# An LSTM step's first half packed into 128 columns of PSUM, and the second half's o + 1 moved to GpSimd

## Chip, core and metric

One core of one Trainium2 chip. The metric is device time in microseconds of the whole kernel: 1992.09 us, the median of three runs (1990.87 to 1992.61).

## What is computed

Input x is 8 sequences of 512 steps and 512 features. An LSTM runs over them and is added to x; a small state space model (a conditioned convolution over the eight last steps, a gated scan with 64 states, a projection back) runs over the result and is added again.

```python
def step(carry, xw_t):                    # 512 times, H = 512, batch 8
    prev_h, prev_c = carry
    a = xw_t + prev_h @ Wh                # Wh: 512 x 2048
    i = sigmoid(a[:, :H]); f = sigmoid(a[:, H:2*H]); o = sigmoid(a[:, 2*H:3*H])
    g = tanh(a[:, 3*H:])
    next_c = f * prev_c + i * g
    next_h = o * tanh(next_c)
x = x + lstm(x, h0=cond[:, :512], Wx, Wh, b)
proj = (conv_b + causal_conv(x, taps=cond)) @ Wp + bp
state_t = decay * state + dt * softplus(proj[..., :64]) * (x @ Ws + bs)
x = x + (tanh(proj[..., 64:]) * state_t) @ Wo + bo
```

## The kernel before

The 512 steps of the LSTM are a chain: each needs the h of the one before. Everything else (the projection of x by Wx, the convolution, the scan, the output) is cut into small jobs that are written into the steps, beside the chain. Plain Python lists fix ahead of time which job stands in which step (`project_at`, `conv_when`, `post_at`, `out_when`); every engine then executes its own instructions strictly in the order written, and semaphores join them.

One step splits the 512 hidden units into four chunks of 128 and these into two halves: half 0 (called A, bank recA, chunks 0 and 1) and half 1 (B, recB, chunks 2 and 3). Each half goes through the same stages:

- ScalarE (`seeds`, L626) writes the projected x of the step into the PSUM bank, scaled by a mask that keeps the rows of this step and sets the others to zero. Two steps lie in one row of `seed`.
- TensorE (`recur`, L465) adds h @ Wh. h is the stationary operand, 16 columns: 8 sequences times a high and a low f16 part (they fill 16 rows). Wh moves, also split into a high and a low part (`whi`, `wlo`), 256 columns at a time (two chunks of 128). The 128 rows of the bank are four quadrants of 32, one for each j; in each quadrant 16 rows are used and 16 are empty. For each chunk k of the previous h there are 2 x 4 = 8 matmuls per half, so 32 in a half and 64 in a step. The order of the step is A k=0, A k=1, B k=0, A k=2, A k=3, B k=1, 2, 3. Chunks 0 and 1 wait for the previous step's h of half A (`s_h[0]`), chunks 2 and 3 for that of half B (`s_h[1]`); the first also waits for the seed.
- VectorE transposes blocks of 32 x 32 (`open_`, L812: 128 x 256), adds the rows of the high and low part of h (`add`, L818), and later forms i * g and f * c (`product`, L823) and c (`cell`, L828).
- ScalarE makes tanh of all gates (`gates`, L699; the sigmoid is taken from tanh) and tanh of c (`tanh_c`, L709).
- o + 1 times a constant: for half A on GpSimd (L400), for half B on ScalarE (`opened`, L705).
- GpSimd multiplies it by tanh of c, h in f32 (L406). VectorE makes the high f16 part of h (`high`, L834) and, from GpSimd's h, the low part (`low`, L840), which releases the next step's matmuls.

The orders within a step, which the engines keep:

```python
# VectorE (then beside(t))
open_(t, 0); add(t, 0); open_(t, 1); product(t, 0); add(t, 1); cell(t, 0)
product(t, 1); high(t, 0); cell(t, 1); low(t, 0); high(t, 1); low(t, 1)
# ScalarE (then beside(t))
gates(t, 0); seeds(t + 1, 0); gates(t, 1); tanh_c(t, 0); opened(t); seeds(t + 1, 1); tanh_c(t, 1)
```

TensorE runs its beside(t) after all 64 matmuls of the step: L435 and L432 (projection), L510 (convolution), L483, L523, L530 (output). The DMA queue of SyncE brings the projected rows back from a scratch in HBM (`rows_back`, L336), four transfers for each tile and half.

The functions in full:

Of the kernel before, what the change touches and what calls it, by code (L numbers as in the profile page):

```python
# [5 lines left out]
def lstm_ssm_kernel(nc: bass.Bass, x, cond, Wx, Wh, b, conv_b, Wp, bp, Ws, bs, A_log, dt_log, Wo, bo, out):  # L6
    f32 = mybir.dt.float32
    f32r = mybir.dt.float32r
    f16 = mybir.dt.float16
    bf16 = mybir.dt.bfloat16  # L10
    i32 = mybir.dt.int32
    ALU = mybir.AluOpType
# [19 lines left out]
    with ctx:  # L32
# [18 lines left out]
        mask = sb("mask", [128, 2])  # L51
        yt = sb("yt", [128, XR, KC, ROW])
        h32 = sb("h32", [128, KC, HS, NB])
        hb = [sb(f"hb{i}", [128, KC, 2 * NB], f16) for i in range(2)]
        h0b = [sb(f"h0b{i}", [128, KC, 2 * NB], bf16) for i in range(2)]
# [18 lines left out]
        tr = [sb(f"tr{h}", [128, 2, G, 4, NB]) for h in range(2)]  # L74
# [82 lines left out]
        brow = [xs[z:z + 1, :, :].rearrange("p c n -> p (c n)") for z in (0, 32)]  # L157

# [151 lines left out]
        def _(sync):  # L310
# [14 lines left out]
            def rows_back(g, c, z):  # L325
# [8 lines left out]
                back = scratch[g % 2, c, :, :].rearrange("(t q) (j f) -> j q t f", q=2 * NB, j=4)  # L334
                for j in range(4):
                    sync.dma_start(seed[32 * j:32 * j + 2 * NB, z, :, c // 2, 128 * (c % 2):128 * (c % 2) + 128],  # L336
                                   back[j, :, TS // 2 * z:TS // 2 * z + TS // 2, :]).then_inc(s_seedin[z], 16)
# [43 lines left out]
        def _(pool):  # L381
# [16 lines left out]
            for t in range(T):  # L398
                pool.wait_ge(s_tg[0], t + 1)
                pool.tensor_scalar(osc[0][:, :], act[0][:, 2, :], 1.0, SC, ALU.add, ALU.mult).then_inc(s_os[0], 1)  # L400
                for q in range(2):
                    pool.wait_ge(s_tc[q], t + 1)
# [8 lines left out]
        def _(pe):  # L411
# [43 lines left out]
            def recur(t, half, k):  # L455
# [6 lines left out]
                for h in (h0b if t == 0 else [hb[(t - 1) % 2]]):  # L462
                    for w in (whi, wlo):
                        for j in range(4):
                            ins = pe.matmul(rec[half][32 * j:32 * j + 2 * NB, 0:256].rearrange("p (c f) -> p c f", c=2),  # L465
                                            h[:, k, :],
                                            w[:, k, :, :].rearrange("p (c j) f -> p c j f", j=4)[:, 2 * half:2 * half + 2, j, :],
                                            start=False, stop=(k == KC - 1), skip_group_check=True)
# [123 lines left out]
        def _(act_eng):  # L592
# [29 lines left out]
            def seeds(t, q):  # L622

                if t % TS == 0 and q == 0:
                    act_eng.wait_ge(s_seedin[t // TS % 2], 256 * (t // TT + 1))
                act_eng.activation(rec[q][:, 0:256], seed[:, t // TS % 2, t % TS // 2, q, :],  # L626
                                   ACT.Copy, scale=mask[:, t % 2:t % 2 + 1]).then_inc(s_seed[q], 1)
# [74 lines left out]
            def opened(t):  # L702

# [380 lines left out]
```

## Time and profile before

| what | value |
|---|---|
| median of three runs | 1992.09 us |
| the profiled execution's own time | 1992.87 us |
| its span | 1991.0 us |
| mean granted TensorE clock | 0.987 of 2.4 GHz |
| PE busy | 1791.8 us, 90%, 36290 matmuls |
| VectorE busy | 1430.1 us, 72%, 6913 instructions |
| ScalarE busy | 1043.9 us, 52%, 4056 instructions |
| GpSimd busy | 349.4 us, 18%, 1546 instructions |

The busy times are of one execution. Matmuls are pipelined, the time of one reaches from its start to its last result, and those of neighbours overlap, so 90% isn't a full engine. Four matmuls that go to the four quadrants start almost at once and stand in the timeline as one row, "x4". PE, PEld, DVE, ACT and POOL are matmuls, weight loads, VectorE, ScalarE and GpSimd. An idle time in brackets at the end of a row names what ended it.

### The profile page before, as it was taken

What the parts mean: (1) busy time and instruction counts of PE and PEld (TensorE: products, weight loads), DVE (VectorE), ACT (ScalarE), POOL (GpSimd) and SP (SyncE); (2) the same over time, 40 slices, a digit from 0 to 9 for tenths busy, and PEclk for the clock granted to TensorE, in tenths of its full rate; (3) what the DMA queues carried; (4) which work ended last, traced back from release to release, by engine and by line L of the source; (5) the groups of instructions that cost most, each with busy time, mean ns of one, the idle gap of its engine ahead of it and who ended that gap; (6) DMA issues with size and microseconds to landing.
All of it is one profiled execution on the core that took longest, in us unless ns stands there. A gap on an engine that the chain in (4) does not pass through costs nothing.

```text
span 1991.0 us, 90455 instructions
## 1 busy us (share of the span) xinstructions
PE 1791.8 (90%) x36290; PEld 1282.6 (64%) x36290; DVE 1430.1 (72%) x6913; ACT 1043.9 (52%) x4056; POOL 349.4 (18%) x1546
## 2 busy tenths in 40 slices
PE   2688899999999999999999999999999999999976
PEld 1455666666666666666666666766666677666755
DVE  4577666777777777777767777777777777767775
ACT  3355555555555555555555555555555555555452
POOL 3011111111111111111111111111111111111110
PEclk8799999999999999999999999999999999999998
DMA  5111111111121111111111111111111111211100
GB/s 201 49 47 44 39 50 36 40 55 48 37 61 49 42 45 51 49 41 58 46 48 46 44 46 51 53 49 49 46 39 51 50 52 34 66 45 40 47 17 23
DMA packets 112284, 98.71 MB, mean 50 GB/s; under 512 B 20097, under 2 KB 86197, under 8 KB 110838
## 3 DMA queue, kind: packets, MB, share of 16 engines
q1 hardware_dynamic: 111490, 92.35, 15.3%
q8 instruction: 286, 4.69, 1.0%
q14 instruction: 134, 1.10, 0.2%
q10 hardware_dynamic: 374, 0.57, 0.1%
HBM read 50.90 MB, written 41.94 MB: 47 GB/s over the span
## 4 chain that ended last, share of the span: by engine, by line
PE 45%; DVE 33%; ACT 11%; issue 5%; POOL 4%; DMA 1%; SPq 0%; ACTq 0%; POOLq 0%; DVEq 0%
PE recA L465 25%; DVE tr L812 16%; PE recB L465 9%; DVE pre L818 7%; ACT act L699 5%; PE pw L435 5%; PE pbc L510 5%; POOL h L406 4%; DVE hb L840 3%; ACT tc L709 3%; DVE prod L823 2%; DMA xs<-in_L_cond_b_dram 1%; ACT recB L626 1%; DVE acc L893 1%; DVE st L914 0%
## 5 line engine op out<-in xcount | busy, mean ns | idle before, releaser
L699 ACT ACTIVATE act<-pre 128x64 f32<-128x64 f32 x1024 | 262.8, 257 | 874.0 <-DVE pre L818 857.6
L465 PE MATMUL recA<-whi,hb 128*16 128x256 f16 x8176 | 514.6, 274 | 137.8 <-DVE hb L840 131.3
L465 PE MATMUL recB<-wlo,hb 128*16 128x256 f16 x8176 | 513.2, 273 | 0.0
L465 PE MATMUL recB<-whi,hb 128*16 128x256 f16 x8176 | 513.2, 273 | 0.0
L465 PE MATMUL recA<-wlo,hb 128*16 128x256 f16 x8176 | 512.9, 273 | 0.0
L465 PEld LDWEIGHTS recA<-whi,hb 128*16 128x16 f16 x8176 | 200.0, 88 | 402.8 <-DVE hb L840 347.1
L812 DVE STREAM_TRANSPOSE tr<-recA 128x256 f32<-128x256 f32 x512 | 229.9, 449 | 215.5 <-PE recA L465 214.3
L510 PE MATMUL pbc<-yt,wpk 128*128 128x256 f32 (+5 forms) x1120 | 333.7, 402 | 0.0
L406 POOL TENSOR_TENSOR h<-osc,tc 128x16 f32<-128x16 f32 x1024 | 227.8, 222 | 500.8 <-ACT tc L709 500.8
L400 POOL TENSOR_SCALAR osc<-act 128x16 f32<-128x16 f32 x512 | 105.0, 205 | 1088.3 <-ACT act L699 1088.3
L823 DVE SCALAR_TENSOR_TENSOR prod<-act 128x32 f32<-128x32 f32 x1024 | 196.7, 192 | 126.4 <-ACT act L699 126.4
L818 DVE TENSOR_TENSOR pre<-tr 128x64 f32<-128x64 f32 x1024 | 229.3, 224 | 17.6
L626 ACT ACTIVATE recA<-seed,mask 128x256 f32<-128x256 f32 x512 | 236.1, 461 | 9.2 <-DMA seed<-xw_rows 9.2
L834 DVE TENSOR_TENSOR hb<-osc,tc 128x16 f16<-128x16 f32 x1024 | 178.1, 174 | 85.2 <-ACT tc L709 83.7
L626 ACT ACTIVATE recB<-seed,mask 128x256 f32<-128x256 f32 x512 | 236.1, 461 | 0.0
L435 PE MATMUL pw<-wxh,xh 128*128 128x512 f32 x504 | 228.0, 452 | 6.6 <-DVE wxl L785 5.8
L812 DVE STREAM_TRANSPOSE tr<-recB 128x256 f32<-128x256 f32 x512 | 230.0, 449 | 1.8 <-PE recB L465 1.8
L840 DVE TENSOR_TENSOR hb<-h,hb 128x16 f16<-128x16 f32 x1024 | 179.5, 175 | 70.8 <-POOL h L406 3.7
L510 PEld LDWEIGHTS pbc<-yt,wpk 128*128 128x128 f32 x1120 | 169.9, 190 | 90.6 <-issue 85.8
L435 PE MATMUL pw<-wxh,xl 128*128 128x512 f32 x504 | 219.6, 436 | 0.0
L465 PEld LDWEIGHTS recB<-wlo,hb 128*16 128x16 f16 x8176 | 204.7, 90 | 19.2
L465 PEld LDWEIGHTS recB<-whi,hb 128*16 128x16 f16 x8176 | 204.7, 90 | 19.1
(150 smaller groups left out, 2051.7 us busy)
## 6 DMA issues: line engine op xcount, KB each, us to landing
xw_rows<-xs SPq DMA_DIRECT2D x128, 256.0 KB, 2.1
seed<-xw_rows SPq DMA_DIRECT2D x1024, 32.0 KB, 1.9
out_dram<-ot SPq DMA_DIRECT2D x32, 256.0 KB, 3.0
xn<-in_x_dram SPq DMA_DIRECT2D x30, 256.0 KB
seed<-in_L_cond_Wh_dram SPq DMA_DIRECT2D x2, 1024.0 KB, 7.3
wpk<-in_L_cond_Wh_dram SPq DMA_DIRECT2D x2, 1024.0 KB, 14.7
wlo<-in_L_cond_Wx_dram SPq DMA_DIRECT2D x2, 1024.0 KB, 20.2
xs<-in_L_cond_Wx_dram SPq DMA_DIRECT2D x1, 1024.0 KB, 4.9
```

The lines of the kernel that those rows point to most:

```text
L400: pool.tensor_scalar(osc[0][:, :], act[0][:, 2, :], 1.0, SC, ALU.add, ALU.mult).then_inc(s_os[0], 1)
L406: pool.tensor_tensor(h32[:, 2 * q:2 * q + 2, t % HS, :], osc[q][:, :].rearrange("p (c b) -> p c b", c=2), tc[q][:, :].rearrange("p (c b) - ...
L435: pe.matmul(out, xx[:, g % 2, k, :], wxm[w][:, k, c, :, :, :], start=(first and part == 0), stop=False)
L465: ins = pe.matmul(rec[half][32 * j:32 * j + 2 * NB, 0:256].rearrange("p (c f) -> p c f", c=2), h[:, k, :], w[:, k, :, :].rearrange("p (c j ...
L510: ins = pe.matmul(pbc[:, NB * (lo - a):NB * (hi - a)], wpk[:, k, c, :], yt[:, n % XR, c, NB * (lo + k):NB * (hi + k)], start=(j == 0), sto ...
L626: act_eng.activation(rec[q][:, 0:256], seed[:, t // TS % 2, t % TS // 2, q, :], ACT.Copy, scale=mask[:, t % 2:t % 2 + 1]).then_inc(s_seed[ ...
L699: act_eng.activation(act[q][:, 0:G, :].rearrange("p g n -> p (g n)"), pre[q][:, :, :, :].rearrange("p g c b -> p (g c b)"), ACT.Tanh, scal ...
L812: dve.transpose(tr[q][:, :, :, :, :].rearrange("p c g z b -> p (c g z b)"), rec[q][:, 0:256]).then_inc(s_tr[q], 1)
L818: dve.tensor_tensor(pre[q][:, :, :, :].rearrange("p g c b -> p c g b"), tr[q][:, :, :, 0, :], tr[q][:, :, :, 1, :], ALU.add).then_inc(s_ad ...
L823: dve.scalar_tensor_tensor(prod[q][:, :, :], act[q][:, 0:2, :], 1.0, act[q][:, 3:5, :], ALU.add, ALU.mult).then_inc(s_prod[q], 1)
L834: dve.tensor_tensor(hb[t % 2][:, 2 * q:2 * q + 2, 0:NB], osc[q][:, :].rearrange("p (c b) -> p c b", c=2), tc[q][:, :].rearrange("p (c b) - ...
L840: dve.tensor_tensor(hb[t % 2][:, 2 * q:2 * q + 2, NB:2 * NB], h32[:, 2 * q:2 * q + 2, t % HS, :], hb[t % 2][:, 2 * q:2 * q + 2, 0:NB], ALU ...
```

## The change

Half A's two chunks now share a quadrant: chunk c = 0 takes rows 0 to 15 and c = 1 rows 16 to 31, in the same 128 columns. To write one chunk and add nothing to the other's rows, the stationary operand becomes 32 columns wide: h with 16 columns of zeros behind it (c = 0) or ahead of it (c = 1). `hz` and `h0z` hold 16 zero columns on both sides of h for that, and `hb`, `h0b` are now views of their middle. Half A then takes 4 x 2 x 2 x 4 = 64 matmuls of 128 columns (before 32 of 256); half B keeps its 32 of 256. That makes 96 in a step.

With it half A's seed and transpose are 128 columns wide (`WIDTH`), its mask keeps other rows, the transfers that bring the seed back place chunk 1 in rows 16 to 31, and the add reads another order. The o + 1 of half B moves from ScalarE (`opened`, which is gone) to GpSimd, between h of A and h of B. Lines without a change are cut from the diff.

```diff
@@ -48,11 +48,12 @@
         seed = sb("seed", [128, 2, TS // 2, 2, 256])
-        mask = sb("mask", [128, 2])
+        mask = sb("mask", [128, 2, 2])
         yt = sb("yt", [128, XR, KC, ROW])
         h32 = sb("h32", [128, KC, HS, NB])
-        hb = [sb(f"hb{i}", [128, KC, 2 * NB], f16) for i in range(2)]
-        h0b = [sb(f"h0b{i}", [128, KC, 2 * NB], bf16) for i in range(2)]
+        hz = [sb(f"hz{i}", [128, KC, 6 * NB], f16) for i in range(2)]
+        h0z = [sb(f"h0z{i}", [128, KC, 6 * NB], bf16) for i in range(2)]
         h0f = sb("h0f", [128, 2, KC, NB])
@@ -71,7 +72,7 @@
         scale = sb("scale", [128, 4])
-        tr = [sb(f"tr{h}", [128, 2, G, 4, NB]) for h in range(2)]
+        tr = [sb("tr0", [128, G, 2, 2, NB]), sb("tr1", [128, 2, G, 4, NB])]
         pre = [sb(f"pre{h}", [128, G, 2, NB]) for h in range(2)]
@@ -155,6 +156,10 @@
+        hb, h0b = ([h[:, :, 2 * NB:4 * NB] for h in hs] for hs in (hz, h0z))
+        WIDTH = (128, 256)
@@ -332,8 +337,9 @@
                 back = scratch[g % 2, c, :, :].rearrange("(t q) (j f) -> j q t f", q=2 * NB, j=4)
+                row, col = ((2 * NB * c, 0), (0, 128 * (c % 2)))[c // 2]
                 for j in range(4):
-                    sync.dma_start(seed[32 * j:32 * j + 2 * NB, z, :, c // 2, 128 * (c % 2):128 * (c % 2) + 128],
+                    sync.dma_start(seed[32 * j + row:32 * j + row + 2 * NB, z, :, c // 2, col:col + 128],
                                    back[j, :, TS // 2 * z:TS // 2 * z + TS // 2, :]).then_inc(s_seedin[z], 16)
@@ -396,9 +402,10 @@
             for t in range(T):
-                pool.wait_ge(s_tg[0], t + 1)
-                pool.tensor_scalar(osc[0][:, :], act[0][:, 2, :], 1.0, SC, ALU.add, ALU.mult).then_inc(s_os[0], 1)
                 for q in range(2):
+                    pool.wait_ge(s_tg[q], t + 1)
+                    pool.tensor_scalar(osc[q][:, :], act[q][:, 2, :], 1.0, SC, ALU.add, ALU.mult).then_inc(s_os[q], 1)
                     pool.wait_ge(s_tc[q], t + 1)
@@ -459,13 +466,22 @@
-                for h in (h0b if t == 0 else [hb[(t - 1) % 2]]):
-                    for w in (whi, wlo):
-                        for j in range(4):
-                            ins = pe.matmul(rec[half][32 * j:32 * j + 2 * NB, 0:256].rearrange("p (c f) -> p c f", c=2),
-                                            h[:, k, :],
-                                            w[:, k, :, :].rearrange("p (c j) f -> p c j f", j=4)[:, 2 * half:2 * half + 2, j, :],
-                                            start=False, stop=(k == KC - 1), skip_group_check=True)
+                for h in (h0z if t == 0 else [hz[(t - 1) % 2]]):
+                    if half:
+                        for w in (whi, wlo):
+                            for j in range(4):
+                                ins = pe.matmul(rec[1][32 * j:32 * j + 2 * NB, 0:256].rearrange("p (c f) -> p c f", c=2),
+                                                h[:, k, 2 * NB:4 * NB],
+                                                w[:, k, :, :].rearrange("p (c j) f -> p c j f", j=4)[:, 2:4, j, :],
+                                                start=False, stop=(k == KC - 1), skip_group_check=True)
+                    else:
+                        for c in range(2):
+                            for w in (whi, wlo):
+                                for j in range(4):
+                                    ins = pe.matmul(rec[0][32 * j:32 * j + 32, 0:128],
+                                                    h[:, k, 2 * NB * (1 - c):2 * NB * (1 - c) + 32], w[:, k, 4 * c + j, :],
+                                                    start=False, stop=(k == KC - 1), skip_group_check=True)
                 if k == KC - 1:
@@ -623,8 +639,8 @@
                     act_eng.wait_ge(s_seedin[t // TS % 2], 256 * (t // TT + 1))
-                act_eng.activation(rec[q][:, 0:256], seed[:, t // TS % 2, t % TS // 2, q, :],
-                                   ACT.Copy, scale=mask[:, t % 2:t % 2 + 1]).then_inc(s_seed[q], 1)
+                act_eng.activation(rec[q][:, 0:WIDTH[q]], seed[:, t // TS % 2, t % TS // 2, q, 0:WIDTH[q]],
+                                   ACT.Copy, scale=mask[:, q, t % 2:t % 2 + 1]).then_inc(s_seed[q], 1)
@@ -699,11 +715,6 @@
-            def opened(t):
-                act_eng.wait_ge(s_tg[1], t + 1)
-                act_eng.activation(osc[1][:, :], act[1][:, 2, :], ACT.Copy, bias=SC, scale=SC).then_inc(s_os[1], 1)
@@ -748,7 +759,7 @@
             act_eng.wait_ge(s_bits, 2)
-            act_eng.wait_ge(s_mask, 5)
+            act_eng.wait_ge(s_mask, 7)
             for q in range(2):
@@ -758,7 +769,6 @@
                     tanh_c(t, 0)
-                    opened(t)
                     if t + 1 < T:
@@ -809,14 +819,18 @@
                 dve.wait_ge(s_rec[q], t + 1)
-                dve.transpose(tr[q][:, :, :, :, :].rearrange("p c g z b -> p (c g z b)"),
-                              rec[q][:, 0:256]).then_inc(s_tr[q], 1)
+                order = ("p g c z b -> p (g c z b)", "p c g z b -> p (c g z b)")[q]
+                dve.transpose(tr[q][:, :, :, :, :].rearrange(order), rec[q][:, 0:WIDTH[q]]).then_inc(s_tr[q], 1)
                 dve.wait_ge(s_tr[q], t + 1)
-                dve.tensor_tensor(pre[q][:, :, :, :].rearrange("p g c b -> p c g b"), tr[q][:, :, :, 0, :],
-                                  tr[q][:, :, :, 1, :], ALU.add).then_inc(s_add[q], 1)
+                if q:
+                    dve.tensor_tensor(pre[1][:, :, :, :].rearrange("p g c b -> p c g b"), tr[1][:, :, :, 0, :],
+                                      tr[1][:, :, :, 1, :], ALU.add).then_inc(s_add[1], 1)
+                else:
+                    dve.tensor_tensor(pre[0][:, :, :, :], tr[0][:, :, :, 0, :],
+                                      tr[0][:, :, :, 1, :], ALU.add).then_inc(s_add[0], 1)
@@ -966,8 +980,8 @@
                 dve.memset(act[q][:, 4, :], 0.0).then_inc(s_c[q], 1)
-                dve.memset(hb[q][:, :, :], 0.0)
-                dve.memset(h0b[q][:, :, :], 0.0).then_inc(s_hz, 1)
+                dve.memset(hz[q][:, :, :], 0.0)
+                dve.memset(h0z[q][:, :, :], 0.0).then_inc(s_hz, 1)
             dve.memset(ones[:, :].bitcast(f32), 1.0).then_inc(s_hz, 1)
@@ -975,7 +989,9 @@
             for z in range(2):
-                dve.tensor_reduce(mask[:, z:z + 1], diag[:, z:16:4], mybir.AxisListType.X, ALU.max).then_inc(s_mask, 1)
+                for q in range(2):
+                    dve.tensor_reduce(mask[:, q, z:z + 1], diag[:, z:16:2 + 2 * q], mybir.AxisListType.X,
+                                      ALU.max).then_inc(s_mask, 1)
@@ -1009,7 +1025,7 @@
             dve.wait_ge(s_max, KC + 1)
-            dve.wait_ge(s_mask, 3)
+            dve.wait_ge(s_mask, 5)
             dve.tensor_scalar(diag[:, :], ident[:, :], top[:, 4:5], None, ALU.mult).then_inc(s_max, 1)
@@ -1030,8 +1046,8 @@
             dve.wait_ge(s_scale, 1)
-            for z in range(2):
-                dve.tensor_scalar(mask[:, z:z + 1], mask[:, z:z + 1], scale[:, 2:3], None, ALU.mult).then_inc(s_mask, 1)
+            for q in range(2):
+                dve.tensor_scalar(mask[:, q, :], mask[:, q, :], scale[:, 2:3], None, ALU.mult).then_inc(s_mask, 1)
             wh_high(2)
```

## Rows read from the trace of the kernel before

**Rows 1.** The page: chain by line, then two groups (busy us, mean ns of one).

```profile
PE recA L465 25%; DVE tr L812 16%; PE recB L465 9%; DVE pre L818 7%; ACT act L699 5%; PE pw L435 5%; PE pbc L510 5%; POOL h L406 4%; DVE hb L840 3%; ACT tc L709 3%; DVE prod L823 2%; DMA xs<-in_L_cond_b_dram 1%; ACT recB L626 1%; DVE acc L893 1%; DVE st L914 0%
...
L465 PEld LDWEIGHTS recA<-whi,hb 128*16 128x16 f16 x8176 | 200.0, 88 | 402.8 <-DVE hb L840 347.1
...
L400 POOL TENSOR_SCALAR osc<-act 128x16 f32<-128x16 f32 x512 | 105.0, 205 | 1088.3 <-ACT act L699 1088.3
```

**Rows 2.** Chain in order of time, one step (start us, us, what).

```profile
1011.24 0.46 DVE tr L812
...
1011.95 0.40 DVE tr L812
```

**Rows 3.** Timeline of that step, PE (start us, us, engine, line, operation).

```profile
1009.92 0.29 PE L465 MATMUL recA<-whi,hb 128*16 128x256 f16 x4
...
1010.47 0.28 PE L465 MATMUL recB<-wlo,hb 128*16 128x256 f16 x4
1010.56 0.10 PEld L465 LDWEIGHTS recA<-whi,hb 128*16 128x16 f16 x4
1010.58 0.28 PE L465 MATMUL recA<-whi,hb 128*16 128x256 f16 x4
...
1010.91 0.28 PE L465 MATMUL recA<-wlo,hb 128*16 128x256 f16 x4
...
1011.56 0.28 PE L465 MATMUL recB<-wlo,hb 128*16 128x256 f16 x4
```

**Rows 4.** Same timeline, the other engines, to the next step's weights.

```profile
1011.24 0.45 DVE L812 STREAM_TRANSPOSE tr<-recA 128x256 f32<-128x256 f32 x1 [0.73 <-PE recA L465]
...
1011.73 0.22 DVE L818 TENSOR_TENSOR pre<-tr 128x64 f32<-128x64 f32 x1
...
1011.90 0.45 DVE L812 STREAM_TRANSPOSE tr<-recB 128x256 f32<-128x256 f32 x1
...
1012.15 0.46 ACT L626 ACTIVATE recA<-seed,mask 128x256 f32<-128x256 f32 x1
...
1012.38 0.22 DVE L818 TENSOR_TENSOR pre<-tr 128x64 f32<-128x64 f32 x1
1012.53 0.17 DVE L828 SCALAR_TENSOR_TENSOR act<-prod 128x16 f32<-128x16 f32 x1
...
1012.64 0.26 ACT L699 ACTIVATE act<-pre 128x64 f32<-128x64 f32 x1
...
1012.80 0.20 ACT L709 ACTIVATE tc<-act 128x16 f32<-128x16 f32 x1
1012.93 0.22 ACT L705 ACTIVATE osc<-act 128x16 f32<-128x16 f32 x1
...
1013.05 0.46 ACT L626 ACTIVATE recB<-seed,mask 128x256 f32<-128x256 f32 x1
1013.08 0.22 POOL L406 TENSOR_TENSOR h<-osc,tc 128x16 f32<-128x16 f32 x1 [0.55 <-ACT tc L709]
...
1013.34 0.18 DVE L840 TENSOR_TENSOR hb<-h,hb 128x16 f16<-128x16 f32 x1
1013.45 0.20 ACT L709 ACTIVATE tc<-act 128x16 f32<-128x16 f32 x1
1013.57 0.10 PEld L465 LDWEIGHTS recA<-whi,hb 128*16 128x16 f16 x4 [0.63 <-DVE hb L840]
```

**Rows 5.** Timeline where step 0 begins, PE.

```profile
72.91 0.13 PEld L465 LDWEIGHTS recA<-whi,h0b 128*16 128x16 bf16 x4 [10.90 <-issue]
72.94 0.39 PE L465 MATMUL recA<-whi,h0b 128*16 128x256 f16 x4 [10.49 <-ACT recA L626]
```

**Rows 6.** Timeline of the last stage, PE.

```profile
1972.62 0.69 PE L483 MATMUL pu<-yt,ws 128*64 128x64 f32 x16 [0.83 <-DVE yt L849]
1973.23 4.08 PE L510 MATMUL pbc<-yt,wpk 128*128 128x8 f32 x32
```

**Rows 7.** Waits of the whole run (us in total, times, longest us).

```profile
DVE tr L812 <- PE recA L465: 214.3, 453, 13.1
```

## The prediction

> **What bounds the kernel now.** I read the page's chain first, then the same chain in order of time, then the timeline of one plain step, and last the groups by form. The page gives the recurrence's matmuls into recA 25% of the chain, the transpose of L812 16%, recB 9% [rows 1]. In order of time one step reads: recA's matmuls, transpose A, add A, transpose B [rows 2]. Taken at its word, transpose A (0.46 us a step) sits on the path, and the change halves it. Whether it does sit there is the main question of this case.
>
> The timeline answers it. Call the first matmul of a step 0; it is 1009.92, and the next step's weight load is at 1013.57, so a step lasts 3.65 us. PE works in groups of four matmuls (j = 0 to 3) that start together, one group each 0.109 us: from 1010.58 to 1011.56 are nine intervals, 0.98 us [rows 3]. The order is A (chunks 0, 1), B (0), A (2, 3), B (1 to 3). The last A group starts at 1010.91 and runs 0.28, to 1011.19; transpose A starts at 1011.24, 0.05 later. The last B group starts at 1011.56, ends at 1011.84, and transpose B starts at 1011.90, 0.06 later [rows 3, 4]. Both transposes lag the end of their own matmuls by the same hand-over. Transpose B starts before add A has ended (1011.73 + 0.22 = 1011.95), 0.17 after add A started; VectorE can do that in 0.15 (add B 1012.38, cell A 1012.53) [rows 4]. So transpose B waits for PE, and the path of a step is: all sixteen groups (1.64 to the start of the last one, 0.28 for it), hand-over 0.06, transpose B 0.45, add B, gates B, tanh of c A (behind gates B on ScalarE; cell A, 1012.53 + 0.17 = 1012.70, was ready 0.10 before it), h of A on GpSimd, low part of A, next step's weights: 1011.90, 1012.38, 1012.64, 1012.80, 1013.08, 1013.34, 1013.57 [rows 4]. Transpose A and add A lie beside the B matmuls with about 0.02 us to spare (0.17 against 0.15). The chain view names them because they come just before transpose B on the same engine.
>
> **The change part by part.**
>
> *PE, first half.* Before: 8 groups of 256 columns, 8 x 0.109 = 0.872 us. After: 16 groups of 128 columns. The group of 256 columns takes 256 / 2.4 GHz = 0.107 us at the upper of TensorE's two clocks, and the rows show 0.109, so 0.0023 us come with each group. With 128 columns that is 0.0533 + 0.0023 = 0.0556 us, an estimate, and 16 of them are 0.890: 0.018 us longer in each step. The columns streamed are the same, the group's fixed part is paid twice. Bounds for the group, which the trace doesn't show for four tiles of 128 columns: below, 0.0533 (no fixed part, 0.019 us a step less than now); above, 0.109 as now (each matmul keeps its slot whatever its width, 0.872 us a step more). Which is nearer? The four matmuls of a group start within 0.01 us of each other and the four weight loads together take 0.10 us where one takes 0.09 [rows 1, 3], so tiles don't queue behind each other. The sixteen 64-column matmuls of L483, in pairs of two tiles, took 0.69 us with the last one's 0.23 in it: 0.46 us / 7 = 0.066 us a pair [rows 6]. So a group of well under 0.109 exists, and I take 0.0556.
>
> *Weight loads of 32 columns instead of 16.* 32 loads of 128-column weights with 8-column matmuls (where nothing but the weight can bind) took 4.08 us, 0.127 us each or about 0.032 us per 32 columns [rows 6]; a load starts while the group before streams. 0.032 is under 0.0556, so it is hidden, if the four tiles load side by side, as above. Only the first group of a step, which finds an idle array, shows it: 0 to 0.032, I take 0.007. Cost at nothing otherwise; if the four loads were serial the group would be 4 x 0.032 = 0.128, worse than the upper bound.
>
> *PE's queue.* 192 instead of 128 instructions (weights and matmuls) for a step's recurrence. The sequencer is free to run ahead from the seed of A on (that is the wait ahead of the first weights): seed A 1012.15 + 0.46 = 1012.61, the next weights 1013.57, 0.96 us ahead [rows 4]; after the change the seed ends about 0.2 earlier. In step 0, where the seed comes last, eight instructions start within 0.04 us of the first weight load [rows 5], 0.005 us each. Needed are eight per 0.0556, 0.007 each. I take no cost; the other end is the second rival.
>
> *VectorE.* Transpose A falls from 128x256 to 128x128. It took 0.45; the add with 64 columns takes 0.22 [rows 4], so 192 columns make 0.23 and 128 make 0.15, and about 0.30 is left. It lay beside the B matmuls, so this brings nothing in a plain step: next late is transpose B, which PE holds. In 512 - 453 = 59 steps VectorE came late to transpose A [rows 7]; there the shorter one gives back up to 0.15 each, 8.9 us at most, and since most of these are late by less or are late elsewhere too, I take 3 us. Add A has the same 64 results, only another order of reading: 0.22 as before.
>
> *ScalarE.* The seed of A falls by some 0.1 us, and the Copy that makes o + 1 of B (0.22, 1012.93) goes. Neither is on the path: A's tanh of c comes ahead of both the Copy and seed B. What moves is B's tanh: seed B starts 0.12 earlier (it followed the Copy at 1013.05), and then c of B is what is late. That makes B's h up to 0.1 us earlier; but PE takes chunks 2 and 3 at 1010.58, exactly one group interval (0.11) after the group at 1010.47 [rows 3], so B's h wasn't waited for. Gain 0. Bounds: 0 to -0.02, since it was just in time.
>
> *GpSimd.* It now makes o + 1 of B after h of A: h A ends 1013.08 + 0.22 = 1013.30, the new one (0.205 as its twin for A [rows 1]) then ends at about 1013.55. B's tanh, then 0.12 earlier than 1013.45, ends near 1013.55 as well. Behind the new wait on GpSimd stands h of B, and its low part and recA's chunks 2 and 3 wait for that. If o + 1 came 0.1 later than I have it, the high part would be where it is now. Cost 0, other end 0.05.
>
> *The rest.* DMAs keep their number and size. Masks, memsets (192 instead of 64 columns) and waits ahead of step 0 lie beside loads of Wx. 0, at most 1 us.
>
> **Sum**, against the profiled run's own 1992.87 us (span 1991.0): 512 x (0.018 + 0.007) = +12.8, late steps -3, in all +10, 2003. The median of the runs shown is 0.8 lower, so 2002 us.
>
> **A rule of the skill against this change.** The rows show four matmuls starting within 0.01 us [rows 3], and 0.109 / 4 = 0.027 us on average. The Trainium skill, TensorE: Matmul & The Clock Gate, "Wait — 56ns, not 53.3ns?", says that starts of consecutive matmuls are never less than about 25 ns apart however narrow they are. By that rule a group of four would take 0.100 us, an estimate from that page, and the change would cost 16 x 0.100 - 0.872 = 0.73 us a step, some 370 us. This case's starts inside a group contradict it as a spacing, but its average would just fit, so it stays as the third rival. The same page's "Part 3: Packing small matmuls" has tiles starting about 4 ns apart, and there the rows agree.
>
> **The rivals.**
> 1. *VectorE's order was the bound.* Then transpose A was on the path, as [rows 2] reads, and 0.15 x 512 = 77 us go: 1915. Against it: transpose B's 0.06 behind recB's end, and 0.17 where 0.15 does. It decides only if transpose B could start before PE is done, which it can't. Milder: the fixed part of a group vanishes at 128 columns and the late steps give all: 512 x -0.019 - 5 = -15 us, 1977.
> 2. *PE's sequencer can't feed the packed half.* If an instruction costs 0.0125 us (a little under the 0.109 / 8 = 0.0136 at which it is consumed now) and the queue holds what A's chunks 0 and 1 need, the 80 instructions from B's chunk 0 to A's last leave from about 0.22 us on, when the first have ended: 0.22 + 80 x 0.0125 = 1.22, needed at 1.06. That is 0.16 us a step, 82 us: 2074. Against it: the burst of [rows 5]. It decides from 0.0105 us an instruction.
> 3. *Each matmul keeps its slot.* Group 0.109: 0.872 us x 512 = 446 us, 2438. For it: nowhere in the trace are matmuls denser than 0.027 each on average. Against it: 64-column pairs, and the starts within a group.
> 4. *Nothing to be measured* (within 0.2%, 4 us, about what a measurement of this kernel can tell): the group at 0.054 to 0.055 or late steps giving more.
>
> **How the numbers follow.** Forecast (slower by 4 to 45 us) 0.52; rival 4 0.14; rival 1 in both forms 0.16; rival 2 and anything like it 0.12; rival 3 0.06. Faster 0.16, same 0.14, slower 0.52 + 0.12 + 0.06 = 0.70. The range reaches from the mild form of rival 1 to rival 2, 1978 to 2076, and leaves out the strong form of rival 1 and rival 3, with 0.09 and 0.06, and something of the edges. The forecast's own range is 1996 to 2037: its upper end is a group of 0.058 with 0.03 for the first one's weights.
>
> **What would show it right or wrong.** A's groups 0.055 to 0.056 apart; the last B group starting 1.66 to 1.67 after the step's first; transpose B still 0.05 to 0.06 behind recB's end, transpose A at about 0.30 with VectorE idle behind add A; a plain step of 3.67 to 3.68; h A, low A and the next weights at the same distances as in [rows 4]. Wrong would be: A's groups at 0.1 (rival 3), gaps in the second half of recA (rival 2), transpose B starting earlier than now counted from the step's first matmul (rival 1), or GpSimd's new o + 1 ending what h B waits for.

## The result, and the profile after

The changed kernel takes 2007.1 us, median of 4 runs (2006.48 to 2008.14); the kernel before takes 1991.48 us, median of 4 (1989.47 to 1992.61; the three runs shown and one more beside the changed kernel). The ratio is 1.0076, interval 1.0064 to 1.0089: slower, by 15 us. The forecast was 2002.0, slower, and the range of 1978 to 2076 holds the time.

The profiled execution after took 2008.14 us with a span of 2006.3, against 1992.87 and 1991.0 before: 15.3 us more. A plain step, as the median distance between the first matmuls of two steps, is 3.676 us, where it was 3.650. The last 511 steps make 0.026 x 511 = 13.3 of the 15.3.

The page after, its chain and three groups of it:

```profile
PE recA L482 26%; PE recB L474 22%; DVE tr L823 8%; PE pw L442 5%; PE pbc L526 5%; ACT act L715 5%; POOL h L413 4%; DVE pre L829 4%; DVE hz L854 3%; ACT tc L720 2%; DVE prod L837 2%; DMA xs<-in_L_cond_b_dram 1%; PE po L546 0%; PE po L539 0%; DVE acc L907 0%
...
L482 PE MATMUL recA<-whi,hz 128*32 128x128 f16 x16352 | 582.4, 220 | 137.8 <-DVE hz L854 131.3
L482 PEld LDWEIGHTS recA<-whi,hz 128*32 128x32 f16 x16352 | 404.3, 96 | 396.2 <-DVE hz L854 351.1
...
L408 POOL TENSOR_SCALAR osc<-act 128x16 f32<-128x16 f32 x1024 | 207.8, 203 | 1071.6 <-ACT act L715 1028.5
```

The chain names recB with 22% and the transposes with 8%, where it was 9% and 16% [rows 1]. That looks like work which moved from VectorE to TensorE. It isn't: experiment 3, below, shows the same exchange with no change in time. GpSimd's o + 1 now stands with 1024 instructions instead of 512.

The timeline of a plain step after, all engines, to the second half's high part in the next step:

```profile
1009.37 0.10 PEld L482 LDWEIGHTS recA<-whi,hz 128*32 128x32 f16 x4 [1.50 <-DVE hz L854]
1009.38 0.24 PE L482 MATMUL recA<-whi,hz 128*32 128x128 f16 x4 [1.09 <-DVE hz L854]
...
1009.44 0.23 PE L482 MATMUL recA<-wlo,hz 128*32 128x128 f16 x4
...
1009.50 0.23 PE L482 MATMUL recA<-whi,hz 128*32 128x128 f16 x4
...
1009.83 0.28 PE L474 MATMUL recB<-whi,hz 128*16 128x256 f16 x4
...
1010.05 0.23 PE L482 MATMUL recA<-whi,hz 128*32 128x128 f16 x4
...
1010.44 0.23 PE L482 MATMUL recA<-wlo,hz 128*32 128x128 f16 x4
...
1010.72 0.32 DVE L823 STREAM_TRANSPOSE tr<-recA 128x128 f32<-128x128 f32 x1 [0.35 <-PE recA L482]
...
1011.04 0.28 PE L474 MATMUL recB<-wlo,hz 128*16 128x256 f16 x4
1011.07 0.22 DVE L832 TENSOR_TENSOR pre<-tr 128x64 f32<-128x64 f32 x1
...
1011.38 0.45 DVE L823 STREAM_TRANSPOSE tr<-recB 128x256 f32<-128x256 f32 x1
1011.49 0.36 ACT L642 ACTIVATE recA<-seed,mask 128x128 f32<-128x128 f32 x1
...
1011.86 0.23 DVE L829 TENSOR_TENSOR pre<-tr 128x64 f32<-128x64 f32 x1
...
1012.12 0.26 ACT L715 ACTIVATE act<-pre 128x64 f32<-128x64 f32 x1 [0.27 <-DVE pre L829]
...
1012.28 0.20 ACT L720 ACTIVATE tc<-act 128x16 f32<-128x16 f32 x1
...
1012.57 0.22 POOL L413 TENSOR_TENSOR h<-osc,tc 128x16 f32<-128x16 f32 x1 [0.69 <-ACT tc L720]
...
1012.82 0.18 DVE L854 TENSOR_TENSOR hz<-h,hz 128x16 f16<-128x16 f32 x1
1012.85 0.22 ACT L720 ACTIVATE tc<-act 128x16 f32<-128x16 f32 x1
1012.87 0.20 POOL L408 TENSOR_SCALAR osc<-act 128x16 f32<-128x16 f32 x1
1013.05 0.10 PEld L482 LDWEIGHTS recA<-whi,hz 128*32 128x32 f16 x4 [0.37 <-DVE hz L854]
...
1013.18 0.18 DVE L848 TENSOR_TENSOR hz<-osc,tc 128x16 f16<-128x16 f32 x1 [0.18 <-POOL osc L408]
```

Read it against [rows 3, 4]. A's groups start at 1009.38, .44, .50, one each 0.0555 us. The first group of recA's second half starts at 1010.05, in place after B's chunk 0. The last group of A starts at 1010.44, the last of B at 1011.04, 1.67 after the step's first weights, where it was 1.64. Transpose A takes 0.32 and add A ends at 1011.29; VectorE then has nothing of the recurrence to do until 1011.38, 0.06 behind the end of recB's last group (1011.04 + 0.28). From there on the distances are those of [rows 4]: transpose B to add B 0.48, gates B 0.26 later, tanh of c A 0.16, h A 0.29, low part 0.25, next weights 0.23. Seed A (1011.49) takes 0.36 instead of 0.46, off the path.

New is the last line: the high part of B waits for GpSimd. GpSimd's h of A ends at 1012.79, its o + 1 of B starts at 1012.87 and ends at 1013.07, just when B's tanh (1012.85 + 0.22) ends. The high part starts at 1013.18, 0.11 behind both; in [rows 4] the tanh of B ended at 1013.65 and the high part followed 0.03 later, at 1013.68:

```profile
1013.68 0.17 DVE L834 TENSOR_TENSOR hb<-osc,tc 128x16 f16<-128x16 f32 x1 [0.17 <-ACT tc L709]
```

Over all steps the medians are 0.10 from the end of o + 1 to the high part, and 0.03 before, from the end of the tanh.

The waits of the whole run after (us in total, times, longest us):

```profile
DVE tr L823 <- PE recA L482: 219.5, 452, 12.3
...
DVE hz L848 <- POOL osc L408: 91.9, 496, 0.6
```

The first row is that of [rows 7], a transpose A that PE held in 452 steps instead of 453. The second had no counterpart: in 496 of 512 steps VectorE's high part of B comes behind GpSimd's o + 1.

### The profile page after: what moved, and what is told of

The parts are those of the page before. It is cut to its first block, busy times and chain, and to the rows that moved or that the text cites. A ratio compares the mean times of both kernels' runs of the same rounds, so it can differ in the third digit from the quotient of the medians.

```text
span 2006.3 us, 123289 instructions
## 1 busy us (share of the span) xinstructions
PE 1806.9 (90%) x52706; PEld 1334.9 (67%) x52706; DVE 1388.8 (69%) x6915; ACT 953.7 (48%) x3544; POOL 451.3 (22%) x2058
## 4 chain that ended last, share of the span: by engine, by line
PE 59%; DVE 20%; ACT 10%; POOL 5%; issue 5%; DMA 1%; SPq 0%; ACTq 0%; POOLq 0%; DVEq 0%
PE recA L482 26%; PE recB L474 22%; DVE tr L823 8%; PE pw L442 5%; PE pbc L526 5%; ACT act L715 5%; POOL h L413 4%; DVE pre L829 4%; DVE hz L854 3%; ACT tc L720 2%; DVE prod L837 2%; DMA xs<-in_L_cond_b_dram 1%; PE po L546 0%; PE po L539 0%; DVE acc L907 0%
## 5 line engine op out<-in xcount | busy, mean ns | idle before, releaser
L482 PE MATMUL recA<-whi,hz 128*32 128x128 f16 x16352 | 582.4, 220 | 137.8 <-DVE hz L854 131.3
L482 PEld LDWEIGHTS recA<-whi,hz 128*32 128x32 f16 x16352 | 404.3, 96 | 396.2 <-DVE hz L854 351.1
L482 PE MATMUL recA<-wlo,hz 128*32 128x128 f16 x16352 | 576.8, 219 | 0.0
L474 PE MATMUL recB<-whi,hz 128*16 128x256 f16 x8176 | 512.8, 273 | 0.0
L474 PE MATMUL recB<-wlo,hz 128*16 128x256 f16 x8176 | 512.8, 273 | 0.0
L482 PEld LDWEIGHTS recA<-wlo,hz 128*32 128x32 f16 x16352 | 436.9, 97 | 0.1
L854 DVE TENSOR_TENSOR hz<-h,hz 128x16 f16<-128x16 f32 x1024 | 179.2, 175 | 73.7 <-POOL h L413 8.9
L442 PE MATMUL pw<-wxl,xh 128*128 128x512 f32 x504 | 215.5, 428 | 0.0
L720 ACT ACTIVATE tc<-act 128x16 f32<-128x16 f32 x1024 | 212.3, 207 | 2.5 <-DVE act L842 2.4
L474 PEld LDWEIGHTS recB<-wlo,hz 128*16 128x16 f16 x8176 | 204.8, 90 | 9.7 <-issue 0.3
```

What stands on the lines that cost most here:

```text
L442: pe.matmul(out, xx[:, g % 2, k, :], wxm[w][:, k, c, :, :, :], start=(first and part == 0), stop=False)
L474: ins = pe.matmul(rec[1][32 * j:32 * j + 2 * NB, 0:256].rearrange("p (c f) -> p c f", c=2), h[:, k, 2 * NB:4 * NB], w[:, k, :, :].rearrang ...
L482: ins = pe.matmul(rec[0][32 * j:32 * j + 32, 0:128], h[:, k, 2 * NB * (1 - c):2 * NB * (1 - c) + 32], w[:, k, 4 * c + j, :], start=False, ...
L720: act_eng.activation(tc[q][:, :], act[q][:, 4, :], ACT.Tanh, scale=0.5).then_inc(s_tc[q], 1)
L854: dve.tensor_tensor(hb[t % 2][:, 2 * q:2 * q + 2, NB:2 * NB], h32[:, 2 * q:2 * q + 2, t % HS, :], hb[t % 2][:, 2 * q:2 * q + 2, 0:NB], ALU ...
```

## Experiments

All ratios are against the kernel before on the same chip, from medians, with a 95% interval. The chips differ a little: the kernel before took 1991.94 us beside experiments 1 to 4, 1993.82 beside 5 to 8 and 1995.39 beside 9 to 12. "..." stands for lines left out, in the code too.

**1 and 2. The two parts alone.** The packing without the move:

```diff
+                pool.wait_ge(s_tg[0], t + 1)
+                pool.tensor_scalar(osc[0][:, :], act[0][:, 2, :], 1.0, SC, ALU.add, ALU.mult).then_inc(s_os[0], 1)
                 for q in range(2):
-                    pool.wait_ge(s_tg[q], t + 1)
-                    pool.tensor_scalar(osc[q][:, :], act[q][:, 2, :], 1.0, SC, ALU.add, ALU.mult).then_inc(s_os[q], 1)
...
+            def opened(t):
...
+                act_eng.wait_ge(s_tg[1], t + 1)
+                act_eng.activation(osc[1][:, :], act[1][:, 2, :], ACT.Copy, bias=SC, scale=SC).then_inc(s_os[1], 1)
...
+                    opened(t)
```

`opened` is called behind `tanh_c(t, 0)`, as before the change.

> The changed kernel with the o + 1 of half B back on ScalarE, so the packing alone. Theory (all of the change's cost is in PE's stream of matmuls, the move to GpSimd lies beside the path): 2007 us, within 3 us of the changed kernel, a plain step 3.68 us. Rival (the new operation on GpSimd, which now ends what the high part of B's h waits for, costs something): 3 to 13 us less than 2007, down to 1994, with a plain step of 3.65 to 3.67.

2004.52 us, ratio 1.0061 (1.0047 to 1.0075), a plain step of 3.675. Most of the loss, 12.6 us on this chip, is the packing. The move without the packing is the same edit the other way round, on the kernel before:

> The kernel before with only the o + 1 of half B moved from ScalarE to GpSimd. Theory: B's h isn't waited for, so nothing: 1991.5 us, within 3. Rival 1 (GpSimd's operation delays B's h and with it recA's chunks 2 and 3): 1995 to 2005. Rival 2 (B's tanh, 0.12 us earlier behind the shorter ScalarE queue, was on the path): 1930 to 1985.

1997.64 us, ratio 1.0030 (1.0019 to 1.0042). My theory, that it costs nothing, fell; rival 1 of this experiment held. The waits show where:

```profile
DVE hb L828 <- POOL osc L401: 92.9, 497, 0.6
```

B's low part now comes 0.660 after A's instead of 0.642. In a plain step the first group of recA's second half waits 0.004 for it, so the step is 3.654, which makes 2 us in all (with the packing this doesn't show: 3.676 against 3.675). In 22 steps (13 in the kernel before) B's h is more than 0.05 late into recA: these make 5.4 us, before 2.0. Fourteen of the 22 are late by about 0.3; before, four of the 13 were, and the other nine by less than 0.12.

**3 and 4. Halving one transpose in the kernel before.** This asks whether the transposes sit on the path, without touching PE. Experiment 3 (experiment 4 has q == 1 for q == 0):

```diff
+                cut = slice(0, 1 if q == 0 else 2)
-                dve.transpose(tr[q][:, :, :, :, :].rearrange("p c g z b -> p (c g z b)"),
-                              rec[q][:, 0:256]).then_inc(s_tr[q], 1)
+                dve.transpose(tr[q][:, cut, :, :, :].rearrange("p c g z b -> p (c g z b)"),
+                              rec[q][:, 0:128 if q == 0 else 256]).then_inc(s_tr[q], 1)
```

What the transpose no longer fills is set to zero once, ahead of step 0.

> The kernel before with half A's transpose cut to 128 of 256 columns; the second chunk's gates are left at zero, so this leaves out part of the computation. Matmuls, seeds and all else as before. Theory (transpose A lies beside the B matmuls): 1991 us, at most 3 less from steps in which VectorE is late; transpose A 0.32 us, transpose B no earlier in the step. Rival (transpose A is on the path, as the chain of waits reads): 0.13 x 512 = 68 us less, 1923.

1991.16 us, ratio 0.9996 (0.9986 to 1.0005): a shorter transpose A alone brings nothing. VectorE's timeline in experiment 3:

```profile
1001.75 0.32 DVE L813 STREAM_TRANSPOSE tr<-recA 128x128 f32<-128x128 f32 x1 [0.34 <-PE recA L465]
...
1002.10 0.22 DVE L819 TENSOR_TENSOR pre<-tr 128x64 f32<-128x64 f32 x1
...
1002.40 0.45 DVE L813 STREAM_TRANSPOSE tr<-recB 128x256 f32<-128x256 f32 x1
```

Transpose A is 0.32 instead of 0.45, add A ends at 1002.32, and transpose B still starts 0.65 behind transpose A, as in [rows 4] (1011.24, 1011.90): recB is what it waits for. The chain of this kernel:

```profile
by line: PE recA L465 25.3%; PE recB L465 21.9%; DVE tr L813 8.5%; PE pw L435 5.4%; PE pbc L510 5.2%; ACT act L699 5.2%; POOL h L406 4.2%; issue 4.1%; DVE pre L819 3.7%; DVE hb L841 3.5%; ACT tc L709 2.5%; DVE prod L824 1.8%; DMA xs<-in_L_c
```

It names recB with 21.9% and the transposes with 8.5%, the picture of after, at the time of before. So the 16% of [rows 1] came in part from how the chain is read: while add A ended later than PE released transpose B, the view went back along VectorE.

> The kernel before with half B's transpose cut to 128 of 256 columns (part of the computation is left out, as in the run for half A). Transpose B is on the path by every theory, but by mine the product of A stands between it and the add of B: gates A end 0.03 us before the product of A may start, at 2.35 us of the step, and the add of B follows 0.11 later at 2.46, where it is now. So theory: within 5 us of 1991. Rival (nothing stands between): 0.13 x 512 = 68 us less, 1923.

1991.40 us, ratio 0.9994 (0.9985 to 1.0004). Transpose B does start on the path, but 0.13 us less of it brings nothing, for the add behind it is then held by the product of A's cell, which stands ahead of it on VectorE and waits for gates A (transpose B 1001.81 + 0.32, product 1002.19, add B 1002.30). VectorE's timeline in experiment 4, then the product of A's cell in the step of [rows 4]:

```profile
1001.81 0.32 DVE L813 STREAM_TRANSPOSE tr<-recB 128x128 f32<-128x128 f32 x1
...
1002.19 0.19 DVE L824 SCALAR_TENSOR_TENSOR prod<-act 128x32 f32<-128x32 f32 x1
...
1002.30 0.22 DVE L819 TENSOR_TENSOR pre<-tr 128x64 f32<-128x64 f32 x1
```

```profile
1012.27 0.19 DVE L823 SCALAR_TENSOR_TENSOR prod<-act 128x32 f32<-128x32 f32 x1
```

So two ways end together at add B: through recB and transpose B, and through transpose A, add A, gates A and the product. Counted from the step's first weights, the product starts at 2.353 us in the kernel before, at 2.351 with transpose A halved and at 2.353 with transpose B halved, and add B at 2.46 in all three (medians): in the second of these transpose B, ahead of the product on VectorE, holds it, in the third the gates of A do. Neither transpose brings anything alone; a gain takes both, as the undisturbed steps of 3.56 us in experiment 6 show.

**5. Split without packing.** A's matmuls get 128 columns, the weights keep 16, everything else stays as before:

```diff
+                    for c in (range(2) if half == 0 else [None]):
...
+                                    ins = pe.matmul(rec[0][32 * j:32 * j + 2 * NB, 128 * c:128 * c + 128],
+                                                    h[:, k, :], w[:, k, 4 * c + j, :],
+                                                    start=False, stop=(k == KC - 1), skip_group_check=True)
```

> The kernel before with half A's matmuls only split: 64 of 128 columns in place of 32 of 256, each into its own 128 columns of the bank, weights of 16 columns, nothing packed, transposes and seeds as before. Theory (each group of four has a fixed part of about 0.002 us, paid eight times more a step): the last B group 0.02 us later in the step, 512 x 0.02 = +10, 2002 us, between the kernel before and the packing alone (2004.5). Rival (the cost comes from the 32-column weights or from adding into shared rows): 1992, no change.

2003.40 us, ratio 1.0044 (1.0030 to 1.0058); plain step 3.670, the last group of recB 0.020 later than before. Of the packing's 0.025 us a step, 0.020 is the group's fixed part, paid 8 more times: 0.0025 each, as the 0.109 of 256 columns had it (0.0023). What is left, 0.005 to 0.007, comes with the packing and lies in the first group of a step: from its start to that of the second group are 0.066 in the change and 0.059 here, and the groups behind it are alike (0.055 to 0.056). The packing has 32-column weights and shared rows at once; which of them it is wasn't tested.

**6, 7 and 8. Packing the other half.**

Experiments 6 and 8, against the changed kernel (8 has o + 1 of B on ScalarE besides; 7 has PACK = (1,) and is like 8 in this); seed, transpose, add and mask follow PACK in the same way:

```diff
+    PACK = (0, 1)
-                    if half:
+                    if half not in PACK:
...
-                                    ins = pe.matmul(rec[0][32 * j:32 * j + 32, 0:128],
-                                                    h[:, k, 2 * NB * (1 - c):2 * NB * (1 - c) + 32], w[:, k, 4 * c + j, :],
+                                    ins = pe.matmul(rec[half][32 * j:32 * j + 32, 0:128],
+                                                    h[:, k, 2 * NB * (1 - c):2 * NB * (1 - c) + 32], w[:, k, 8 * half + 4 * c + j, :],
```

> The mirror of the change: half B packed, half A as before, o + 1 of B on ScalarE. Theory: transpose B is on the path and falls to 0.32, and PE's stream is 0.02 longer as in the change, but the product of A stands between transpose B and add B on VectorE and starts at 2.35 us of the step as before (it waits for the gates of A), so neither shows: 1992 us, within 4, a plain step 3.65. Rival 1 (PE's longer stream costs what it costs in the change): 2004. Rival 2 (the shorter transpose shows): 13 - 68 = -55, 1937.

1993.15 us, ratio 0.9996 (0.9987 to 1.0005), plain step 3.651. PE's longer stream starts transpose B 0.02 later in the step (1.998 for 1.977), and its shortening hides that, but brings no more. VectorE's timeline:

```profile
1003.22 0.32 DVE L829 STREAM_TRANSPOSE tr<-recB 128x128 f32<-128x128 f32 x1
...
1003.58 0.19 DVE L843 SCALAR_TENSOR_TENSOR prod<-act 128x32 f32<-128x32 f32 x1
...
1003.69 0.22 DVE L838 TENSOR_TENSOR pre<-tr 128x64 f32<-128x64 f32 x1
```

Transpose B ends at 1003.54, 0.13 sooner, and add B starts 0.15 later, behind the product of A's cell (before, the add came 0.03 after the transpose: 1011.90 + 0.45, 1012.38 [rows 4]).

> The changed kernel with half B packed too, 128 matmuls a step. Theory: A's gates now come early enough (transpose A is short), so the product of A is done in time and transpose B's shortening shows in full: step 3.68 + 0.02 - 0.13 = 3.56, 61 us less than the changed kernel, with some of it kept by steps that PE fills: 1953 us (1944 to 1965). Rival 1 (packing costs PE time and brings nothing, as in the change): 2016 to 2020. Rival 2 (PE's sequencer can't feed 256 instructions a step): 2030 and more.

2162.39 us, ratio 1.0841 (1.0821 to 1.0862). My theory, 1953 us, missed by 209 us; the time is that of rival 2. 92 of the 511 steps do take the 3.56 us that I had worked out, but the median is 3.9, and PE's timeline shows why:

```profile
295.20 0.22 PE L483 MATMUL recB<-wlo,hz 128*32 128x128 f16 x2
296.56 0.23 PE L483 MATMUL recB<-wlo,hz 128*32 128x128 f16 x2 [1.14 <-issue]
296.57 0.28 PE L483 MATMUL recB<-whi,hz 128*32 128x128 f16 x4
```

PE stops in the middle of a group of four (two matmuls at 295.20, the other two at 296.56) and waits for no semaphore: the bracket says "issue". The instruction queue in the 1.05 us up to 295.05, and then PE's waits in the whole run:

```profile
q8 instruction: 1, 0.02, 5.5%
```

```profile
PEld recB L483 <- issue: 107.5, 172, 2.2
...
PE recB L483 <- issue: 79.1, 139, 2.3
```

A transfer of the instruction queue ended at 294.99, 0.21 us ahead of the last matmul issued; PE goes on 1.57 us after its end. Between 100 and 1900 us the trace has 274 pauses (over 0.13 us from one matmul's start to the next inside a step, those ahead of recA's second half, where B's h can be late, left out), and they end 1.25 to 1.54 us (5% to 95%) after the last packet of that queue has landed. By the same count the changed kernel has one. The row of that queue (packets, MB) before, after and in experiment 6, from the three pages:

```profile
q8 instruction: 286, 4.69, 1.0%
```

```profile
q8 instruction: 414, 6.78, 1.4%
```

```profile
q8 instruction: 542, 8.88, 1.7%
```

32 x 512 = 16,384 more matmuls, each with its weight load, make 32,768 instructions and 128 more packets: 256 instructions in a packet of 16 KB. With 128 matmuls a step, the recurrence alone takes one packet every 3.56 us; with 96, 256 / 192 x 3.68 = 4.9 us pass for one. In none of the runs do two packets start less than 3.2 us apart. And the pauses keep to the packets' size: with PE's instructions (weight loads, matmuls and waits) numbered in order of time, the one behind a pause has number 193 or 194 in its 256, in all 274 of them.

> Both halves packed, the o + 1 of B on ScalarE. Theory: as with GpSimd's, and B's h without the stalls that GpSimd's second operation brought (2.6 us in the change): 1950 us, 2 to 6 less than with GpSimd. Rival (ScalarE's extra 0.22 us delays B's tanh): equal or up to 10 more than with GpSimd.

2155.14 us, ratio 1.0823 (1.0802 to 1.0844), with 274 such pauses too: this theory fell with the last one, and GpSimd has no part in the stall.

**9. As many matmuls, nothing packed.** Experiment 5's split in both halves of the kernel before:

> The kernel before with the matmuls of both halves split into 128 columns, 128 matmuls a step as with both halves packed, but nothing packed: weights of 16 columns, transposes and seeds as before. Theory (PE runs out of instructions, whatever they are: with both halves packed each pause in a burst of matmuls ended 1.2 to 1.6 us after the start of a 16 KB instruction packet's transfer had ended): pauses again, 2120 to 2190 us against 2013 that the group's fixed part alone would give (512 x 0.04 more). Rival (packing itself pauses PE, by the 32-column weights or the rows shared in PSUM): 2013, no pauses.

2187.13 us, ratio 1.0965 (1.0938 to 1.0993), with 227 pauses by the same count, which end 1.25 to 1.57 us after a packet and again all stand at 193 or 194 of 256 instructions. The theory's range held. PE's wait and the queue's row:

```profile
PEld recB L472 <- issue: 116.7, 167, 2.4
```

```profile
q8 instruction: 542, 8.88, 1.7%
```

So the stall comes with the number of instructions in a step, packed or not, with weights of 16 or of 32 columns.

**10. Both halves packed, back to 96 matmuls.** Against experiment 8:

```diff
-                            for w in (whi, wlo):
+                            for w in ((whi, wlo) if half == 0 else (whi,)):
```

> Both halves packed with the o + 1 of B on ScalarE, but the low f16 part of Wh left out for half B (part of the computation is missing): 96 matmuls a step, as in the change, with both transposes short. Theory (what is wrong with packing both is the supply of instructions alone): no pauses, the step falls to 3.51 us (the product of A, at 2.21, then holds add B at 2.32), 1992 - 69 = 1923 us, at most 1935. Rival (the short transposes bring nothing even so): 1980 to 2000.

1896.08 us, ratio 0.9505 (0.9491 to 0.9520), plain step 3.451, and 14 such pauses where experiment 8 had 274. It isn't a version to use (the expectation says what is left out). It shows that the packed form itself runs well. It came out better than expected (3.51), since B's h is ready when A's second half can first take it: with fewer B matmuls ahead, transpose A starts 1.26 us into the step instead of 1.32, and it is 0.13 shorter, which together is the 0.20 that the step lost. VectorE's timeline:

```profile
1001.82 0.32 DVE L829 STREAM_TRANSPOSE tr<-recA 128x128 f32<-128x128 f32 x1 [0.28 <-PE recA L482]
...
1002.17 0.22 DVE L838 TENSOR_TENSOR pre<-tr 128x64 f32<-128x64 f32 x1
1002.32 0.31 DVE L829 STREAM_TRANSPOSE tr<-recB 128x128 f32<-128x128 f32 x1
...
1002.72 0.19 DVE L843 SCALAR_TENSOR_TENSOR prod<-act 128x32 f32<-128x32 f32 x1
...
1002.83 0.22 DVE L838 TENSOR_TENSOR pre<-tr 128x64 f32<-128x64 f32 x1
```

Now VectorE's bounds show: transpose B starts 0.15 behind add A's start, the closest that an instruction follows an add [rows 4], and 0.21 behind recB's end; add B follows the product of A's cell.

**11 and 12. The change and the packing alone, once more, side by side.**

> The changed kernel, beside the packing alone on one chip, since the two differ by less than their intervals against the kernel before. Theory (the move of o + 1 to GpSimd costs 2 to 4 us, through some ten more steps in which B's h is 0.3 us late): 2007, 2 to 4 more than the packing alone. Rival (it costs nothing): within 1 us of it.

> The packing alone, o + 1 of B on ScalarE, beside the changed kernel on one chip. Theory: 2004 us, 2 to 4 less than the changed kernel. Rival: the same as it.

2009.18 us, ratio 1.0068 (1.0055 to 1.0082), and 2006.88 us, ratio 1.0055 (1.0042 to 1.0069). The intervals overlap; the medians differ by 2.3 us, as 2007.1 and 2004.52 did by 2.6. In the traces the change has 24 steps in which B's h comes late into recA (5.8 us), the packing alone 14 (2.3 us). Beside the packing, GpSimd's move costs 2 to 3 us; alone it cost 5.7 (experiment 2), of which 2 are the plain steps' wait.

## Why the prediction was right, and where it was not

**What bounds the kernel.** Right for this change, and shown: a shorter transpose A alone brings nothing (experiment 3), and transpose B starts 0.052 behind recB's end before and after (medians). The prediction gave transpose A and add A 0.02 us to spare ahead of transpose B; it left out that they also lead over gates A and the product to add B, and there nothing is to spare (experiment 4).

**PE, first half.** The group was estimated at 0.0556 and is 0.055 to 0.056; the last recB group was to be 0.025 later and is 0.027 later (medians), the step 0.026 longer. 0.018 + 0.007 for the first group stands too in the split of experiment 5 (0.020) and the 0.007 by which the first group there and in the change differ. The Trainium skill, TensorE: Matmul & The Clock Gate, "Wait — 56ns, not 53.3ns?", gives a floor of some 25 ns between starts: four matmuls in 0.0555 us are 0.014 each, and they start within 0.010 us, so for matmuls in four column tiles it doesn't hold here, even on average.

**PE's queue.** No cost at 96 matmuls, as forecast, and rival 2 was off for this change. But its kind is real: at 128 matmuls a step it decides (experiments 6 and 9). The argument by [rows 5] was too narrow: a burst of eight instructions shows how fast PE takes what is already there, not how fast new packets come.

**Late steps of VectorE: mis-sized.** Forecast -3 us, measured about -1: the time by which transpose B in such steps lags recB fell from 5.45 to 5.30 us in all, and from transpose B to add B from 6.5 to 5.6.

**ScalarE and GpSimd: the step that failed.** "Cost 0": B's tanh did move up and now ends 0.07 earlier behind h of A (forecast 0.1), but B's h did not come earlier. The estimate had o + 1 end 0.25 behind h of A, with B's tanh, and the high part follow as it did behind the tanh. It ends at 0.29, and the high part comes 0.10 behind it instead of 0.03. These two make the 0.1 of which the prediction said that the high part would then be where it was, and so it is (0.39 behind the end of h of A, before 0.375). B's low part came 0.015 later behind A's (0.657 for 0.642). Plain steps hide that, as forecast.

What the forecast left out is the steps in which B's h is late and PE waits for it in recA: 24 against 13, 5.7 us against 2.0, so +3.7 us. Of the 24, 17 are late by about 0.3, against 4 before and 6 with the packing alone, and they are regular. In 7, exactly 64 steps apart (steps 50, 114, 178 and on to 434), GpSimd's h of B itself starts 0.29 late though its inputs are there; with six instructions a step, waits included, they are 384 = 3 x 128 apart. The move alone has seven such steps too, the packing alone and the kernel before have none. In the other 10, h of B is in time and VectorE's low part starts 0.33 late; counted in VectorE's instructions these ten lie a multiple of 128 apart, to within 2, and so do the four of the kernel before. So on both engines some starts are 0.3 us late at fixed distances in the instructions, and it costs where the instruction has no idle time ahead of it. What happens on the engines at these places, no run shows.

**The sum.** Plain steps give 13.3 us. What the other steps take above a plain one rose from 25.3 to 27.1 us, by 1.8; -1 and +3.7 would be 2.7, and the 0.9 between isn't assigned. With 0.2 outside the steps that makes the 15.3 measured. The forecast had 12.8 - 3 = 10: the plain steps were sized right (12.8 for 13.3), and the 5 us that were missing are the late steps, which didn't get 3 us shorter and brought the waits for B's h. The forecast's three errors, 0.5 on the plain steps, 2 on VectorE's late steps and 3.7 on the waits for B's h, all go the same way, and the 0.9 takes back a part.

## What to carry to other kernels

Before shortening an operation that the chain names, look at what the next one on its engine waits for: if that is another engine's work and follows its end by a bare hand-over, shortening the operation won't start the next one sooner. Then follow its result to where the two ways meet again: when they meet at the same time, as here at add B, only shortening both helps. Splitting matmuls for a neater layout keeps the columns but pays a fixed part for each, and what it buys has to lie on the path. Count the instructions PE takes in a step as well as their columns: a loop can be dense enough that its instructions don't arrive in time.

## What was not expected of the hardware

- **The supply of instructions.** 192 instructions of PE's recurrence in a step of 3.68 us ran with one such pause, where 256 in 3.56 us would have been needed PE stopped 274 times between 100 and 1900 us, for 1.14 us in the row shown and up to 2.3 us. Each stop stood at the same place in a block of 256 instructions, and it ended 1.2 to 1.6 us after a 16 KB packet had landed (experiments 6, 8 and 9). Whether fewer other transfers at that time would help wasn't tried.
- **Four column tiles of 128 columns** start together each 0.0555 us, with 32-column weights at 96 ns each beside them (88 ns for 16 columns [rows 1]).
- **GpSimd back to back**: its next instruction started 0.08 to 0.09 us after the last one's end, with nothing left to wait for. Where it waited for that one's own result (h of B behind o + 1), it was 0.15 us. VectorE's high part started 0.10 us behind the end of GpSimd's o + 1, and 0.03 behind ScalarE's tanh in the kernel before.
- **Late starts at fixed distances.** A start 0.3 us late every 384 instructions of GpSimd (h of B), and on VectorE at multiples of 128 instructions (low parts), in the numbers given with the failed step.
